# One-core attention and MLP block: reordering the start-up, where V's weights, the first normalised tiles and the first MLP weights are made ready

## The chip, the cores and the metric

The kernel runs on one core of a Trainium2 chip. The core has five engines that run side by side, each with its own queue in program order: TensorE (PE, with weight loads shown apart as PEld), VectorE (DVE), ScalarE (ACT), GpSimd (POOL) and SyncE (SP), which here only issues DMAs. They wait for each other through semaphores. The metric is the device time of one execution in microseconds, lower is better; the number given is the median of several runs.

## What is computed

A layer norm without learned scale, then two branches from the same normalised input, and a gated sum. The input has 4 blocks of 512 tokens and 512 features; each block is handled as four tiles of 128 tokens (`TT = 4`).

```python
xn = layernorm(x, eps=1e-5)                      # (x - mean) / sqrt(var + eps), per token
q, k, v = xn @ wq.T, xn @ wk.T, xn @ wv.T        # 16 query heads, 4 key/value heads of 128
s = lightning_attn(rope(q), rope(k), v) @ wo.T   # linear attention with decay, chunks of 64
gate = silu((xn @ f8(gate_w)) * gate_scale)      # f8: rounded to float8_e4m3fn
up = (xn @ f8(up_w)) * up_scale                  # 1536 hidden features
g = silu(((gate * up) @ f8(down_w)) * down_scale)
out = x + s * g
```

The products are made to float32 accuracy from two parts: every operand is split into a high part (a cast to float32r) and a low part (the value minus its high part), and three products high x high, high x low and low x high are summed (`SPLIT`). For the weights that are exactly float8 values, two products do.

## The kernel before

The program has a long first phase for V and the MLP and a second for attention. The change lies in the first 50 us or so, the start-up, and in nothing else.

**Normalising.** A tile of 128 tokens is loaded (`load_x`), `tile_stats` takes its statistics, `mean_var` aggregates them and adds epsilon for a group of tiles (`LGROUPS`), GpSimd's `power` raises the variance to -1/2, and `inv_std` makes one Newton step of three short instructions on VectorE. `norm` then subtracts and scales in place (L876). TensorE transposes the tile into a PSUM bank (`ln_transpose`, four matmuls against the identity), ScalarE casts it to the high part (`norm_hi`) and VectorE subtracts to make the low part (`norm_lo`). The first eight tiles, two blocks, go through this in the start-up.

**V.** The weights of V come in four slices (`wv_tab`, k = 0 to 3) and are split by `wv_split_hi` on ScalarE and `wv_split_lo` on VectorE. For each of the first four tiles V is summed in three parts of four matmuls: `v_first_high` (high x high), `v_first_low` (low input) and `v_first_rest` (low weights). Tiles 4 to 7 do the twelve in one go (`v_tile`). `v_round` and `v_rest` split the result, and `store_v` writes it to HBM from a ring of slots (`VFIRST`).

**MLP weights.** They come as 12 slabs m = 0 to 11, each with gate, up and down weights; slabs 0 and 1 come in three pieces of 512 columns, the others whole (1536 columns). Rounding to float8 goes: `w_exponent` on VectorE takes the exponent bits into the buffer `mag`, `w_floor` on ScalarE makes them a rounding constant, and `w_round` on VectorE adds and subtracts it (L920, then L925 for gate and up, L929 for down). There is one buffer `mag`, so a slab waits until the one before it has been rounded.

**MLP units.** `gate_up` makes gate and up of one slab for one block in 16 matmuls, `silu_gate` and `fuse` (L937) turn them into the hidden values, `fuse_hi` and GpSimd's `fuse_rest` split these, and `down` uses them two slabs later. Gate and up results rotate through three PSUM banks, and `free_bank` makes TensorE wait until the `silu_gate` or `fuse` of three results ago has read its bank.

The order on each engine is written out by hand, a list of calls per engine; semaphores carry the waits. Warm-up matmuls on zeros (`warm_up`: 14 at the start, 4 more after the first transposes) keep TensorE busy before data is there. The functions that the change touches follow, with the lines of the profile.

## Time and profile before

| | |
|---|---|
| Time, median of 3 runs | 898.89 us (898.34 to 899.41) |
| The profiled execution's own time | 898.42 us |
| Its span in the profile | 896.6 us |
| TensorE busy | 889.5 us, 99% of the span |
| VectorE, ScalarE, GpSimd busy | 655.2, 409.4 and 370.3 us |

The span runs from the first to the last recorded instruction; the execution's own time is 1.8 us longer. The busy time of TensorE is a sum over pipelined matmuls, each shown longer than its distance to the next, so the share says how seldom the engine stands still, not how near it is to its peak.

### The profile page before, as it was taken

The numbers are of one execution on the slowest core, as the hardware profiler recorded it, in microseconds if no ns is written. First come the engines' busy times: TensorE is split into PE (matmuls) and PEld (weight loads), VectorE is DVE, ScalarE is ACT, GpSimd is POOL, SyncE is SP. The second block draws the span as 40 slices with busy tenths as digits, with TensorE's granted clock in tenths as the row PEclk, the third lists the DMA queues.
The fourth block names the chain that finished last, engine by engine and source line by source line (L and its number), as shares of the span: only waits on it lengthen the run. The fifth ranks groups of instructions, "written<-read, shape, count | busy, mean of one in ns | idle before, by whom it ended". The sixth has DMA issues, their size and how long they took to land.

```text
span 896.6 us, 12455 instructions
## 1 busy us (share of the span) xinstructions
PE 889.5 (99%) x4060; PEld 734.0 (82%) x4060; DVE 655.2 (73%) x941; ACT 409.4 (46%) x683; POOL 370.3 (41%) x273
## 2 busy tenths in 40 slices
PE   8999999999999999999999999999999999999998
PEld 5878888888888888888888888888888888888887
DVE  7888896777653257766777867677767678788798
ACT  3443344443533455445355454463554544634432
POOL 1011112122122475636545456365454563553546
PEclk9999999999999999999999999999999999999999
DMA  6694414389650634522534614345335064274844
GB/s 215 201 399 146 170 48 164 142 306 327 246 211 1 212 127 146 185 79 110 187 128 155 224 35 175 102 175 194 103 143 180 19 222 158 100 254 109 293 149 155
DMA packets 86922, 150.08 MB, mean 167 GB/s; under 512 B 38480, under 2 KB 59616, under 8 KB 81504
## 3 DMA queue, kind: packets, MB, share of 16 engines
q1 hardware_dynamic: 86880, 149.55, 48.4%
q8 instruction: 23, 0.38, 0.2%
q14 instruction: 19, 0.16, 0.1%
HBM read 103.38 MB, written 46.15 MB: 167 GB/s over the span
## 4 chain that ended last, share of the span: by engine, by line
PE 90%; DVE 4%; issue 3%; POOL 2%; ACT 1%; DMA 0%; SPq 0%; DVEq 0%; POOLq 0%; ACTq 0%
PE bank L1359 89%; POOL d_r L1295 1%; POOL rot L1304 1%; PE bank L1379 0%; DMA stage<-in_x_nat 0%; DVE d_sb L1151 0%; DVE wst L920 0%; DVE tail_sb L1204 0%; DVE d_sb L1103 0%; DVE tail_sb L1202 0%; DVE d_r L1178 0%; ACT mag L598 0%; DVE acc L1198 0%; PE bank L1415 0%; DVE fz L937 0%
## 5 line engine op out<-in xcount | busy, mean ns | idle before, releaser
L1359 PE MATMUL bank<-xn,aw 128*128 128x512 f32 x960 | 229.1, 390 | 0.0
L1304 POOL TENSOR_TENSOR rot<-rot 128x512 f32<-128x512 f32 x80 | 126.7, 1584 | 233.2 <-DVE rot L1090 233.2
L1359 PEld LDWEIGHTS bank<-xn,aw 128*128 128x128 f32 x960 | 179.0, 188 | 37.3 <-issue 0.7
L1359 PE MATMUL bank<-o_r,ow 128*128 128x512 f32 (+1 forms) x792 | 184.5, 383 | 0.2 <-DVE o_r L1157 0.2
L1295 POOL TENSOR_TENSOR d_r<-d_sb,d_r 128x512 fp32r<-128x512 f32 x126 | 165.6, 1338 | 37.0 <-ACT d_r L762 36.9
L1359 PE MATMUL bank<-xn,gu_w 128*128 128x512 f32 x768 | 179.9, 389 | 0.4 <-DVE fz L937 0.4
L1359 PEld LDWEIGHTS bank<-o_r,ow 128*128 128x128 f32 x792 | 145.5, 188 | 29.8 <-issue 0.6
L1359 PEld LDWEIGHTS bank<-xn,gu_w 128*128 128x128 f32 x768 | 144.1, 188 | 30.7 <-DVE dn_w L929 0.8
L1089 DVE TENSOR_TENSOR rot<-bank,rope 128x512 f32<-128x512 f32 x80 | 55.2, 690 | 100.1 <-ACT rot L747 100.0
L746 ACT COPY rot<-bank 64x512 f32<-64x512 f32 x80 | 46.8, 585 | 156.7 <-PE bank L1359 156.5
L762 ACT CAST d_r<-d_sb 128x512 fp32r<-128x512 f32 x128 | 78.9, 621 | 83.2 <-DVE d_sb L1151 62.3
L1278 POOL TENSOR_TENSOR fsplit<-f_all,fsplit 128x512 fp32r<-128x512 f32 x36 | 49.0, 1367 | 129.1 <-ACT fsplit L620 129.1
L1359 PE MATMUL bank<-fsplit,dn_w 128*128 128x512 f32 x384 | 93.8, 390 | 0.0
L1103 DVE TENSOR_TENSOR d_sb<-rot,q_decay 128x256 f32<-128x256 f32 x64 | 83.6, 1324 | 1.2 <-POOL rot L1304 1.2
L1359 PEld LDWEIGHTS bank<-fsplit,dn_w 128*128 128x128 f32 x384 | 71.8, 188 | 15.5 <-issue 0.3
L1151 DVE TENSOR_TENSOR d_sb<-bank,decay 128x512 f32<-128x512 f32 x96 | 64.0, 684 | 22.5 <-PE bank L1359 21.1
L1359 PE MATMUL bank<-q_r,k_r 128*128 128x512 f32 x288 | 78.4, 391 | 0.0
L1359 PE MATMUL bank<-d_r,v_r 128*128 128x512 f32 (+1 forms) x336 | 76.9, 361 | 0.1
L1359 PEld LDWEIGHTS bank<-d_r,v_r 128*128 128x128 f32 x336 | 57.6, 188 | 13.1 <-POOL d_r L1295 2.3
L1359 PEld LDWEIGHTS bank<-q_r,k_r 128*128 128x128 f32 x288 | 52.9, 188 | 10.7 <-DVE q_r L1096 0.6
L735 ACT CAST q_r<-rot 128x512 fp32r<-128x512 f32 x64 | 39.8, 622 | 40.2 <-POOL rot L1304 39.4
L937 DVE SCALAR_TENSOR_TENSOR f_all<-bank,scale_sb,f_all 128x512 f32<-128x512 f32 x36 | 26.9, 747 | 40.9 <-PE bank L1359 34.9
(91 smaller groups left out, 946.3 us busy)
## 6 DMA issues: line engine op xcount, KB each, us to landing
xn<-xn_split SPq DMA_DIRECT2D x15, 2048.0 KB, 7.7
v_decayed<-vd_split SPq DMA_DIRECT2D x32, 512.0 KB, 3.3
vd_r<-v_decayed SPq DMA_DIRECT2D x16, 1024.0 KB, 7.0
v_r<-v_split SPq DMA_DIRECT2D x16, 512.0 KB, 3.6
wst<-in_mlp_w SPq DMA_DIRECT2D x10, 768.0 KB, 6.0
xn_split<-xn SPq DMA_DIRECT2D x3, 2048.0 KB, 10.5
stage<-in_x_t SPq DMA_DIRECT2D x20, 256.0 KB, 5.1
stage<-in_attn_w SPq DMA_DIRECT2D x4, 1280.0 KB, 5.7
```

The lines of the kernel that those rows point to most:

```text
L735: act.copy(dst, rot1[:, r % RRING, :]).then_inc(qk_hi, 1)
L746: act.copy(rot2[0:ROT, r % RRING, :], ps[ROT:, :])
L762: act.copy(d_r[:, slot(e), 0, :], d_sb[:, slot(e), :]).then_inc(d_hi, 1)
L937: dve.scalar_tensor_tensor(out=f, in0=gu_ps[(2 * u + 1) % 3][:], scalar=scale_sb[:, MT + m:MT + m + 1], in1=f, op0=ALU.mult, op1=ALU.mult) ...
L1089: dve.tensor_tensor(rot1[:, r % RRING, :], proj_bank(n, r)[:], rope[:, 0, :], ALU.mult)
L1103: dve.tensor_tensor(d_sb[:, slot(e), bass.ts(h % 2, HALF)], rot1[:, (h + 1) % RRING, HALF:S], q_decay[:, h, :], ALU.mult).then_inc(q_decay ...
L1151: dve.tensor_tensor(by_head(d_sb[:, slot(e), :]), by_head(sc_ps[t % TRING][:]), decay[:, h0:h0 + nh, i0 - j:i0 - j + ni, :], ALU.mult).the ...
L1278: pool.tensor_tensor(fsplit[:, e % FRING, 1, :], src, fsplit[:, e % FRING, 0, :].bitcast(F32), ALU.subtract).then_inc(f_lo, 1)
L1295: pool.tensor_tensor(d_r[:, slot(e), 1, :], d_sb[:, slot(e), :], d_r[:, slot(e), 0, :].bitcast(F32), ALU.subtract).then_inc(d_lo, 1)
L1304: pool.tensor_tensor(rot1[:, r % RRING, :], rot1[:, r % RRING, :], rot2[:, r % RRING, :], ALU.add).then_inc(qk_sum, 1)
L1359: last = pe.matmul(dst, a, b, start=start and x == 0, stop=stop and x == len(pairs) - 1)
```

## The change

It rearranges the start-up. On SP, V's weight slices are loaded between the first tiles, slab 2 of the MLP weights right after the first slabs, and the tiles of block 2 earlier. On VectorE, the variance group of tiles 0 and 1 becomes two groups of one tile. Three of the eight tiles (3, 6 and 7) are normalised by ScalarE, as x * rstd + (-mean * rstd), for which VectorE makes the new `nmr`. Slabs 1 and 2 get `mag` buffers of their own in `spare`, which lies where block 2's input comes later. V's products of the first tiles are ordered anew on TensorE, with `v_first_rest` taken slice by slice, the four extra warm-up matmuls fall away, and V's ring has six slots in place of four. The rounding of slabs 1 and 2 is interleaved with `fuse` in another order (`FLOW`, `READY`), with `w_round` cut into `w_minus`, `w_out_gu` and `w_out_down`.

```diff
-LGROUPS = [(0, 2), (2, 4), (4, 8), (8, 12), (12, 16)]
+LGROUPS = [(0, 1), (1, 2), (2, 4), (4, 8), (8, 12), (12, 16)]
-VFIRST = 4
+VFIRST = 6
-WARM_MORE = 4
+ON_ACT = (TT - 1, 2 * TT - 2, 2 * TT - 1)
+FLOW = [0, 1, 2, 3, 4, 6, 5] + list(range(7, NPIECES))
...
+        mags = {0: mag[:], 1: spare[:, 0, :], 2: spare[:, 1, :]}
...
@@ sync @@
-            for i in range(TT):
-                load_x(i)
+            load_x(0)
+            load_wv(0)
+            load_x(1)
+            load_wv(1)
             sp.dma_start(ident[:], ident_in).then_inc(ident_sem, 16)
-            for k in range(KT):
-                sp.dma_start(wv_raw[:, k, :], wv_tab[:, k, :]).then_inc(wv_in[k], 16)
-            for i in range(TT, 2 * TT):
+            load_wv(2)
+            load_wv(3)
+            for i in range(2, 2 * TT):
                 load_x(i)
...
-            store_v(0)
             load_w(2)
-            for v in range(1, TT + 1):
+            for v in range(TT + 2):
                 store_v(v)
+            for i in range(2 * TT, 3 * TT):
+                load_x(i)
             load_w(3)
...
@@ scalar @@
+            def norm(i):
+                c = ON_ACT.index(i)
+                act.wait_ge(nmr_d, 1 if c == 0 else 2)
+                act.activation(stage[:, i % XRING, :], stage[:, i % XRING, :], ACT.Identity,
+                               bias=nmr[:, c:c + 1], scale=rstd[:, i:i + 1]).then_inc(normed_act, 1)
...
-            wv_split_hi(0)
+            for k in range(KT - 1):
+                wv_split_hi(k)
             norm_hi(0)
-            for k in range(1, KT):
-                wv_split_hi(k)
-            for i in range(1, TT):
-                norm_hi(i)
+            wv_split_hi(KT - 1)
+            norm_hi(1)
+            norm(TT - 1)
+            norm_hi(2)
+            norm_hi(3)
+            norm(2 * TT - 2)
+            norm(2 * TT - 1)
...
@@ vector @@
+                if grp in (2, 3):
+                    c0, c1 = (0, 1) if grp == 2 else (1, 3)
+                    dve.wait_ge(rstd_d, grp + 1)
+                    dve.scalar_tensor_tensor(out=nmr[:, c0:c1], in0=mv[:, i1 - c1 + c0:i1, 0], scalar=-1.0, in1=rstd[:, i1 - c1 + c0:i1],
+                                             op0=ALU.mult, op1=ALU.mult).then_inc(nmr_d, 1)
...
+            def w_minus(q):
...
+                dve.wait_ge(k_made, FLOW.index(q) + 1)
+                dve.scalar_tensor_tensor(out=wst[:, m % WRING, c0:c1], in0=mag_of(m)[:, c0:c1], scalar=F8_FLOOR,
+                                         in1=wst[:, m % WRING, c0:c1], op0=ALU.add, op1=ALU.subtract).then_inc(k_neg, 1)
...
-            w_exponent(4)
-            for v in range(TT + 2, 2 * TT):
-                v_rest(v)
+            w_exponent(6)
             w_round(4)
             dve.wait_ge(const_in, 16)
             fuse(0, 0)
             w_exponent(5)
+            v_rest(TT + 2)
+            w_minus(6)
+            fuse(1, 0)
+            w_out_gu(6)
+            v_rest(TT + 3)
+            fuse(0, 1)
             w_round(5)
-            w_exponent(6)
-            fuse(1, 0)
-            for m in range(1, MT):
+            w_out_down(6)
+            w_exponent(7)
+            fuse(1, 1)
+            for m in range(2, MT):
...
@@ tensor @@
+            def v_first_rest(k, tiles=range(TT)):
+
+                pe.wait_ge(wv_lo, k + 1)
+                for v in tiles:
+                    mm = pe.matmul(v_bank(v)[:], xn_of(0)[:, 0, k, bass.ts(v, P)], wv[:, 1, k, :], start=False, stop=k == KT - 1)
...
-            warm_up(WARM_MORE)
             v_first_high(0)
+            v_first_low(0)
             v_first_high(1)
+            v_first_rest(0, (0, 1))
+            v_first_low(1)
             ln_transpose(2)
             ln_transpose(3)
-            v_first_low(0)
-            v_first_low(1)
+            v_first_rest(1, (0, 1))
             v_first_high(2)
             v_first_high(3)
             v_first_low(2)
             v_first_low(3)
-            for v in range(TT):
-                v_first_rest(v)
-            for i in range(TT, 2 * TT):
-                ln_transpose(i)
+            v_first_rest(0, (2, 3))
+            v_first_rest(1, (2, 3))
+            v_first_rest(2)
+            ln_transpose(TT)
+            ln_transpose(TT + 1)
+            v_first_rest(KT - 1)
+            ln_transpose(TT + 2)
+            ln_transpose(TT + 3)
```

TensorE's queue at the start, before. L1395 is `warm_up`, L1415 `ln_transpose` (four matmuls a tile), L1379 `v_first_high`, and L1359 the other products of V.

```order
L1415 MATMUL bank<-ident,stage 128x128 x8
L1395 MATMUL bank<-acc 128x512 x4
L1379 MATMUL bank<-wv,xn 128x512 x8
L1415 MATMUL bank<-ident,stage 128x128 x8
L1359 MATMUL bank<-wv,xn 128x512 x8
L1379 MATMUL bank<-wv,xn 128x512 x8
L1359 MATMUL bank<-wv,xn 128x512 x24
L1415 MATMUL bank<-ident,stage 128x128 x16
L1359 MATMUL bank<-wv,xn 128x512 x48
```

The same stretch of the changed kernel, from the end of the second pair of products on; L1481 is `ln_transpose`, L1440 `v_first_high`, L1420 `v_first_low` and later `v_tile`, L1451 `v_first_rest`.

```order
L1440 MATMUL bank<-wv,xn 128x512 x4
L1451 MATMUL bank<-wv,xn 128x512 x2
L1420 MATMUL bank<-wv,xn 128x512 x4
L1481 MATMUL bank<-ident,stage 128x128 x8
L1451 MATMUL bank<-wv,xn 128x512 x2
L1440 MATMUL bank<-wv,xn 128x512 x8
L1420 MATMUL bank<-wv,xn 128x512 x8
L1451 MATMUL bank<-wv,xn 128x512 x8
L1481 MATMUL bank<-ident,stage 128x128 x8
L1451 MATMUL bank<-wv,xn 128x512 x4
L1481 MATMUL bank<-ident,stage 128x128 x8
L1420 MATMUL bank<-wv,xn 128x512 x48
```

Ahead of these rows stand 14 warm-up matmuls, 8 of `ln_transpose`, 4 of `v_first_high` and 4 of `v_first_low`. The number of matmuls of V is the same, 96; four warm-ups are gone, and the last slice's low weights come between the transposes of tiles 5 and 6.

VectorE's queue at the very start, before: L841 is `tile_stats`, L847 and L849 `mean_var`, L857 to L863 `inv_std`, L876 `norm`.

```order
L841 BN_STATS stats<-stage 128x6 x2
L847 BN_AGGR mv<-stats 128x2 x2
L849 TENSOR_SCALAR rs<-mv 128x2
L841 BN_STATS stats<-stage 128x6
L857 TENSOR_TENSOR rs<-rs 128x2
L859 SCALAR_TENSOR_TENSOR rs<-rs 128x2
L863 SCALAR_TENSOR_TENSOR rstd<-rs 128x2
L876 TENSOR_SCALAR stage<-stage,mv,rstd 128x512 x2
```

And in the changed kernel (L873 `tile_stats`, L879 and L881 `mean_var`, L889 to L895 `inv_std`, L913 `norm`).

```order
L873 BN_STATS stats<-stage 128x6
L879 BN_AGGR mv<-stats 128x2
L881 TENSOR_SCALAR rs<-mv 128x1
L873 BN_STATS stats<-stage 128x6
L879 BN_AGGR mv<-stats 128x2
L881 TENSOR_SCALAR rs<-mv 128x1
L889 TENSOR_TENSOR rs<-rs 128x1
L891 SCALAR_TENSOR_TENSOR rs<-rs 128x1
L895 SCALAR_TENSOR_TENSOR rstd<-rs 128x1
L913 TENSOR_SCALAR stage<-stage,mv,rstd 128x512
L889 TENSOR_TENSOR rs<-rs 128x1
```

The statistics of tile 1 still stand ahead of the Newton step and the `norm` of tile 0; what moved is that tile 1's own Newton step now follows the `norm` of tile 0.

VectorE at the first MLP units, before: L913 is `w_exponent`, L920 to L929 `w_round`, L937 `fuse`. The first row is `fuse(0, 0)`, the last `fuse(0, 1)`.

```order
L937 SCALAR_TENSOR_TENSOR fz<-bank,scale_sb,fz 128x512
L913 TENSOR_SCALAR mag<-wst 128x512
L920 SCALAR_TENSOR_TENSOR wst<-mag,wst 128x512
L929 SCALAR_TENSOR_TENSOR dn_w<-mag,wst 128x512
L913 TENSOR_SCALAR mag<-wst 128x1536
L937 SCALAR_TENSOR_TENSOR f_all<-bank,scale_sb,f_all 128x512
L920 SCALAR_TENSOR_TENSOR wst<-mag,wst 128x1536
L925 SCALAR_TENSOR_TENSOR gu_w<-mag,wst 128x1024
L929 SCALAR_TENSOR_TENSOR dn_w<-mag,wst 128x512
L937 SCALAR_TENSOR_TENSOR fz<-bank,scale_sb,fz 128x512
```

And in the changed kernel: L950 is `w_exponent`, L957 `w_minus`, L965 `w_out_gu`, L973 `w_out_down`, L990 `fuse`, L1000 `v_rest`; the first row is again `fuse(0, 0)`.

```order
L990 SCALAR_TENSOR_TENSOR fz<-bank,scale_sb,fz 128x512
L950 TENSOR_SCALAR spare<-wst 128x512
L1000 TENSOR_TENSOR gout<-bank,gout 128x512
L957 SCALAR_TENSOR_TENSOR wst<-spare,wst 128x1536
L990 SCALAR_TENSOR_TENSOR f_all<-bank,scale_sb,f_all 128x512
L965 SCALAR_TENSOR_TENSOR gu_w<-spare,wst 128x1024
L1000 TENSOR_TENSOR gout<-bank,gout 128x512
L990 SCALAR_TENSOR_TENSOR fz<-bank,scale_sb,fz 128x512
L957 SCALAR_TENSOR_TENSOR wst<-spare,wst 128x512
L973 SCALAR_TENSOR_TENSOR dn_w<-spare,wst 128x512 x2
L950 TENSOR_SCALAR mag<-wst 128x1536
L990 SCALAR_TENSOR_TENSOR f_all<-bank,scale_sb,f_all 128x512
```

`fuse(0, 1)` had the whole rounding of slab 2 ahead of it and now has the down piece of slab 1 and of slab 2 behind it; two of V's tiles were split earlier and now stand between.

## Rows read from the trace of the kernel before

**Rows 1.** The page's head and its busy times by engine.

```profile
span 896.6 us, 12455 instructions
PE 889.5 (99%) x4060; PEld 734.0 (82%) x4060; DVE 655.2 (73%) x941; ACT 409.4 (46%) x683; POOL 370.3 (41%) x273
```

**Rows 2.** Chain that ended last, first 100 us: start, length, what.

```profile
51.28 34.74 PE bank L1359 x152
```

**Rows 3.** Timeline of TensorE: start, length, instructions, idle before them and its releaser.

```profile
1.47 5.89 PE L1395 MATMUL bank<-acc 128*128 128x512 bf16 x14 [1.47 <-DVE acc L981]
8.77 1.06 PE L1415 MATMUL bank<-ident,stage 128*128 128x128 f32 x8 [1.41 <-DVE stage L876]
9.67 1.03 PE L1395 MATMUL bank<-acc 128*128 128x512 bf16 x4
10.34 2.96 PE L1379 MATMUL bank<-wv,xn 128*128 128x512 f32 x8
...
25.17 11.18 PE L1359 MATMUL bank<-wv,xn 128*128 128x512 f32 x48
...
51.28 7.54 PE L1359 MATMUL bank<-xn,gu_w 128*128 128x512 f32 x32 [0.42 <-DVE fz L937]
...
60.47 7.42 PE L1359 MATMUL bank<-xn,gu_w 128*128 128x512 f32 x32
67.72 1.98 PE L1359 MATMUL bank<-fsplit,dn_w 128*128 128x512 f32 x8
```

**Rows 4.** TensorE's weight loads, groups by line, 10 to 14 us.

```profile
L1379 PEld LDWEIGHTS bank<-wv,xn 128*128 128x128 f32 x8 | 1.4, 187 | 1.3 <-ACT wv L638 0.7 <-ACT xn L576 0.3
```

**Rows 5.** Stretches: busy us (instructions) of PE, PEld, DVE, ACT, POOL; granted clock; DMA share, GB/s.

```profile
8.77:25.17 16.40, 16.24 (x85) 12.75 (x85) 14.36 (x37) 7.66 (x15) 1.71 (x2) 1.00 0.50 173
25.17:51.28 26.11, 25.69 (x112) 20.98 (x113) 23.11 (x36) 10.91 (x18) 1.29 (x1) 1.00 0.87 269
```

**Rows 6.** Timeline of VectorE, columns as in rows 3.

```profile
3.99 0.69 DVE L841 BATCH_NORM_STATS2 stats<-stage 128x6 f32<-128x512 f32 x1 [2.58 <-DMA stage<-in_x_nat]
5.41 0.69 DVE L841 BATCH_NORM_STATS2 stats<-stage 128x6 f32<-128x512 f32 x1 [0.73 <-DMA stage<-in_x_nat]
...
6.42 0.17 DVE L849 TENSOR_SCALAR rs<-mv 128x2 f32<-128x2 f32 x1
...
7.49 0.16 DVE L857 TENSOR_TENSOR rs<-rs 128x2 f32<-128x2 f32 x1 [0.30 <-POOL rs L1272]
...
8.08 1.00 DVE L876 TENSOR_SCALAR stage<-stage,mv,rstd 128x512 f32<-128x512 f32 x2
...
16.81 2.47 DVE L841 BATCH_NORM_STATS2 stats<-stage 128x6 f32<-128x512 f32 x4
...
58.08 0.95 DVE L913 TENSOR_SCALAR mag<-wst 128x1536 int32<-128x1536 int32 x1
```

**Rows 7.** Timeline of ScalarE, columns as in rows 3.

```profile
8.48 0.62 ACT L638 CAST wv<-f_all 128x512 fp32r<-128x512 f32 x1 [6.46 <-DMA f_all<-in_wv_tab]
9.43 0.59 ACT L576 CAST xn<-bank 128x512 fp32r<-128x512 f32 x1 [0.32 <-PE bank L1415]
...
27.34 1.34 ACT L598 ACTIVATE mag<-mag,floor_b 128x512 f32<-128x512 f32 x2 [1.47 <-DVE mag L913]
```

**Rows 8.** Timeline of GpSimd, columns as in rows 3.

```profile
6.74 0.71 POOL L1272 TENSOR_TENSOR rs<-rs,minus_half 128x2 f32<-128x2 f32 x1 [5.86 <-DVE rs L849]
...
19.97 1.01 POOL L1272 TENSOR_TENSOR rs<-rs,minus_half 128x4 f32<-128x4 f32 x1 [9.02 <-DVE rs L849]
```

**Rows 9.** SP's issues of tiles 1 and 2 (1.2 to 2.0 us).

```profile
L310 SPq DMA_DIRECT2D stage<-in_x_nat x2: 422/422/423, 1.2 to 1.7; - x2
...
DMA to landing us min/median/max: 4.2/4.3/4.4
```

**Rows 10.** SP's issues of slabs 3 and 4 (39 to 46 us).

```profile
L343 SPq DMA_DIRECT2D wst<-in_mlp_w x2: 352/518/685, 39.4 to 45.5; - x2
...
DMA to landing us min/median/max: 5.2/5.6/6.0
```

More of the change, by code:

```diff
@@ L68 @@
 VSLOT = 2
-VFIRST = 4
+VFIRST = 6
+VUSES = [(2 * TT - r + VFIRST - 1) // VFIRST for r in range(VFIRST)]
 SPILL = 4
@@ L85 @@
 WARM = 14
-WARM_MORE = 4
+ON_ACT = (TT - 1, 2 * TT - 2, 2 * TT - 1)
+FLOW = [0, 1, 2, 3, 4, 6, 5] + list(range(7, NPIECES))
+READY = [(0, 0), (0, 1), (1, 0), (1, 1), (0, 2), (2, 1), (1, 2), (2, 2)] + [(m, part) for m in range(3, MT) for part in (1, 2)]
 EXP_MASK = 0x7F800000
@@ L276, in ready @@
         def ready(m, down=False):
-            if m < SLABS:
-                return 2 * SLABS + m + 1 if down else 2 * m + 2
-            return PARTS * SLABS + 2 * (m - SLABS) + (2 if down else 1)
+            return READY.index((m, 2 if down else 1)) + 1
         def slot(e):
@@ L413, in _ @@
             spill_xn(0)
-            for i in range(2 * TT, 3 * TT):
-                load_x(i)
             load_w(5)
@@ L687, in _ @@
             silu_gate(1, 0)
-            w_floor(6)
             for m in range(1, MT):
@@ L999, in _ @@
             norm_lo(3)
+            for i in range(TT, 2 * TT):
+                tile_stats(i)
+            mean_var(3)
             wv_split_lo(2)
             wv_split_lo(3)
-            for i in range(TT, 2 * TT):
-                tile_stats(i)
-            mean_var(2)
-            inv_std(2)
-            for i in range(TT, 2 * TT):
-                norm(i)
+            inv_std(3)
+            norm(TT)
+            norm(TT + 1)
+            norm_lo(TT)
+            norm_lo(TT + 1)
             v_rest(0)
-            for i in range(TT, 2 * TT):
-                norm_lo(i)
+            norm_lo(TT + 2)
+            norm_lo(TT + 3)
             w_exponent(0)
@@ L1279, in fuse_rest @@
                                    ALU.subtract).then_inc(f_lo, 1)
-            power(0)
-            power(1)
-            power(2)
+            for grp in range(4):
+                power(grp)
             for m in range(MT):
@@ L1286, in _ @@
                 if m in GROUP_AT:
-                    power(GROUP_AT[m] + 1)
+                    power(GROUP_AT[m])
             fuse_rest(MT)
```

124 lines of the change are left out of this document (75 added, 49 removed).

## The prediction

> **What bounds the kernel now.** I read the page first, then the chain that ended last, then TensorE's timeline of the start. TensorE is busy for 889.5 of 896.6 us [rows 1], so all the time in which it stands still is 7.1 us, and the change can't win more than a part of that plus the matmuls it removes. The chain shows one unbroken piece of TensorE from 51.28 us on, 34.7 us long [rows 2], and after it the same rhythm goes on: a unit pair and a down product take 60.47 to 67.72 and so on, 32 matmuls in 7.25 us, 0.2266 us each [rows 3]. The change touches only what is made ready before that. So the question is at which time TensorE comes to the row that now starts at 51.28; every later row moves with it.
>
> In the start the reader should see where TensorE loses time [rows 3, 5]. The first transposes start at 8.77, after 1.41 us of waiting for `norm` of tile 0. From 8.77 to 25.17 TensorE has 48 products of V and 32 transposes. The products cost 48 x 0.2266 = 10.9 us; eight transposes take 1.06 us with the tail of the last one, 0.27 long as the others, so they follow each other at 0.113 us and 32 cost 3.6. That is 14.5 of 16.40 us [rows 5]: 1.9 are lost. About 0.9 are the four warm-ups (from the row at 9.67 to the next, at 10.34, and what they push), 1.0 is waiting for ScalarE's casts of V's weights and of tile 1 in the row at 10.34, which takes 2.96 us for 8 products; the weight loads name both releasers [rows 4]. From 25.17 to 51.28 there are 112 products, 25.4 us, in 26.1 [rows 5]: 0.7 is lost, of which 0.42 shows as the wait for VectorE's `fuse(0, 1)` at the end [rows 3]; the rest of the 0.7 I take as partly the same stop, since the end of the matmul ahead is modelled.
>
> **Part 1, the start.** Transfers of 256 KB land in the order of their issue. Tile 0 is first before and after: statistics at 3.99 [rows 6]. Tile 1 moves from second to third place, behind a slice of V's weights. In the trace the second lands for the statistics at 5.41 [rows 6]; the third, issued at 1.7, has the longer landing of the two, 4.4 us, so 6.1 [rows 9]. VectorE still has tile 1's statistics ahead of tile 0's Newton step, so it waits there until 6.1. From statistics to the variance it took 1.01 us with two aggregations (5.41 to 6.42), with one about 0.9: 7.0. GpSimd's power for tile 0 is long done by then: variance at about 4.9, then 0.3 to its start and at most 0.71 [rows 8]. The Newton step follows at once and takes 0.59 (7.49 to 8.08) [rows 6], so `norm(0)` starts at 7.65 where it was 8.08: 0.4 us earlier, and the transposes of tile 0 at 8.35 in place of 8.77. Splitting the group gains only that: the wait of 0.30 for GpSimd [rows 6] goes, and 0.7 of the later landing eats most of the rest of what one tile alone could have given.
>
> Tile 1 pays: its own Newton step now stands behind `norm(0)`, so `norm(1)` is at 7.65 + 0.46 + 0.57 = 8.7 (it was about 8.5), and TensorE, done with tile 0 at 8.8, waits until 9.4. New wait, 0.6.
>
> **Part 2, V's weights and order.** The slices now take places 2, 4, 6 and 7. The sixth place lands at 8.48 (the first slice of before) [rows 7]. ScalarE casts slices 0 to 2 by 9.0, then tile 0's high part, 9.0 plus the 0.9 us that lay between 9.43 and TensorE's next product [rows 3, 7]: 9.9, a wait of 0.1 behind the transposes of tile 1. After that the weights are there, and the 18 products up to `v_first_low(1)` run without the stops of before, to 14.0. The four warm-ups are gone, and the 1.0 of waiting too: 1.9 removed.
>
> **Part 3, the rest of V's first half.** Each new place where VectorE or ScalarE is late, walked with the durations of before. The group of tiles 2 and 3: its statistics stand behind tile 0's low part, its variance at 11.9, GpSimd 0.3 + 0.71, Newton 0.57 and `nmr` 0.1, `norm(2)` 13.65, transposes 14.3: wait 0.3. Then the cast of tile 2 behind its transposes: wait 0.2. The third slice's low part stands behind four statistics (2.47 us, at 16.81 before and about there now) [rows 6] and the aggregation: it is ready at 20.7 against 20.4: wait 0.3. Last, tiles 4 to 7: variance 19.9, GpSimd 1.01 for four columns [rows 8], Newton, `nmr`, `norm(4)` at 21.8, transposes at 22.5, with TensorE there at 21.6: wait 0.9. Here the kernel before had the products of V's low weights in front and no wait. Sum of new waits: 0.6 + 0.1 + 0.3 + 0.2 + 0.3 + 0.9 = 2.4.
>
> So TensorE reaches tile 4's `v_tile` at 8.35 + 14.5 + 2.4 = 25.2, against 25.17. The earlier start (0.4) and the removed 1.9 are used up by the new waits of 2.4, to within 0.1. The reason is that `norm(4)` hardly moves: VectorE is busy for 14.36 of the 16.40 us [rows 5], the same statistics, splits and Newton steps are in front of it, and three normalisations given to ScalarE (0.46 each) save VectorE only what stands behind `norm(2)` and `norm(5)`, plus three small steps more for the extra group and two for `nmr`.
>
> Costs not in the trace. ScalarE's normalisation of a tile with a scale and a bias per partition: below it the cast from SBUF, 0.62, above it an activation with such a bias, (1.34 + 0.10) / 2 = 0.72 [rows 7]; I take 0.72. With either, TensorE is still on tile 2's transposes or waits 0.1 for tile 3; the sum changes by less than 0.1. A power of one column: two cost 0.71 and four 1.01 [rows 8], so 0.56 as a line through both, 0 to 0.71 as bounds; hidden under the wait for tile 1. The Trainium skill (ScalarE: Activation LUTs, Table sets: the hidden batching unit) says that the cheap functions, identity among them, stand in every table set, so no table is loaded for it; no row of before shows an identity, and a load would show as its own row. The same page (What ACT_TABLE_LOAD costs) prices such an activation at an estimated 0.80 us, by which the sum loses 0.02 more.
>
> **Part 4, the second half and the MLP weights.** From 25.2 the 112 products need 25.4 us: 50.6. What made TensorE wait at 51.28 was `fuse(0, 1)` behind the rounding of slab 2; now it stands in front of slab 1's last piece and is done about 3 us before it is needed, and slab 2's gate weights at about 45.4 against 50.6. So the 0.7 is won, if nothing else is late; of it I count 0.6, since small issue gaps were part of it.
> Slab 4 is late next: its load waits for the end of slab 1's rounding, which now comes at about 49.3, so the load moves from 45.5 [rows 10] by 4 us. With the landing of 5.2 to 6.0 us [rows 10] it is there at 54.5 to 55.3; VectorE wants it at about 56.6 (58.08 before) [rows 6]. Cover left: 1.3 us. Behind that wait would stand `fuse(1, 2)`, which TensorE needs only some 5 us later, so a load late by 2 us costs nothing.
>
> **Sum.** 0.0 at 25.2 plus 0.6 at 51 us: 0.6 us. The profiled execution would go from 898.42 to 897.8 (span 896.0), the median, 0.47 above that execution, from 898.89 to 898.3. A change of 0.2% (1.8 us) is about what can be told from none.
>
> **The rivals.**
> A, the forecast: 0.2 to 1.0 us won, 897.9 to 898.7. Chance 0.70.
> B, tile 1 is later than third place suggests, or the weight slices are. If it lands as the fourth, at about 7.2, the transposes start 0.7 us after 8.77 in place of 0.4 before, and the chain behind them shifts: 1.1 us less, so 0.5 lost, 899.4. If it landed as early as 5.4, 0.7 more would be won, 897.6. For it speaks the same bandwidth for all; against it that sizes and places are alike. Chance of the loss 0.12.
> C, the new waits don't come, because VectorE's queue runs ahead more than my walk says. With none of the 2.4 left, 0.6 + 2.4 = 3.0 us are won, 895.9. It needs `norm(4)` at 20.9 or earlier, and VectorE's fill speaks against it. Over 1.8 us: 0.06; between: 0.04.
> D, the other side: TensorE falls to its lower clock. The 14 first warm-ups took 5.89 us, 0.42 each, where V's products of as many columns take 0.23 [rows 3]: that is the level of 1.2 GHz against 2.4, though the granted clock is shown as 1.00 in the later stretches [rows 5]. Before, warm-ups filled the place between the transposes and the first product; now there are stops of 1.0, 0.6 and 0.1 us around eight transposes. If the lower level came back, each product costs 0.2 more: it decides from 9 products on (1.8 us over, with the gain used up, 12), and 20 of them give 4 - 0.6 = 3.4 lost, 902.3. Against it: before, 1.41 us without work ahead of the transposes did not bring it back. Chance 0.05.
> The Trainium skill (TensorE: Matmul & The Clock Gate, What you observe) says that the default is the throttled state and that idleness brings it back; the trace agrees only for the start, and here no longer stop than before is added.
> E, the weights are late: the load of slab 4 and those behind it meet the two spills of 2 MB. From 5 us of lateness on TensorE waits as long as they are late beyond that; 7 us late would cost 2, 900.9. Chance 0.03.
>
> **How the numbers follow.** A, the small part of C, and B lie within 0.2%: 0.86. Faster 0.06 (C), slower 0.08 (D, E). The range takes A, B on both sides, and the spread of the runs shown (about half a microsecond either way): 897.2 to 899.5.
>
> **What would show it.** `norm(0)` at 7.65; a wait of 0.6 between the transposes of tiles 0 and 1; a wait of about 0.9 before those of tile 4; `v_tile` of tile 4 at 25.2; no wait at 51; the 32 products of block 0 and 1 of slab 2 at about 50.6. I am wrong if TensorE reaches `v_tile` before 24.5 or after 26, or if a wait stands in the slabs 2 to 5.

## The result, and the profile after

The changed kernel takes 899.86 us (median of 21 executions, 898.66 to 901.50) against 898.51 for the kernel before in the same comparison (21 executions, 897.84 to 900.11): ratio 1.0014, interval 1.0008 to 1.0020. It is slower by 1.35 us where 0.6 us faster was forecast, and outside the range given (897.2 to 899.5) by 0.4. Five executions in the comparisons below took 1273 to 2631 us, far above all others of the same kernels; they are left out of every median and count here. The profiled execution took 900.24 us, 2.0 more in its span than before [rows 1].

The head of the page after, with the busy times by engine:

```profile
span 898.6 us, 12452 instructions
PE 889.7 (99%) x4056; PEld 734.5 (82%) x4056; DVE 655.9 (73%) x944; ACT 411.5 (46%) x686; POOL 371.6 (41%) x274
```

TensorE has the same work, less four warm-ups, yet the same busy time. Its timeline after (start, length, instructions, idle before them and its releaser):

```profile
1.47 5.98 PE L1458 MATMUL bank<-acc 128*128 128x512 bf16 x14 [1.47 <-DVE acc L1034]
9.77 0.63 PE L1481 MATMUL bank<-ident,stage 128*128 128x128 f32 x4 [2.32 <-DVE stage L913]
10.71 1.12 PE L1481 MATMUL bank<-ident,stage 128*128 128x128 f32 x4 [0.32 <-DVE stage L913]
...
25.16 1.11 PE L1481 MATMUL bank<-ident,stage 128*128 128x128 f32 x8 [0.92 <-DVE stage L913]
...
27.83 11.14 PE L1420 MATMUL bank<-wv,xn 128*128 128x512 f32 x48
38.81 21.92 PE L1420 MATMUL bank<-xn,gu_w 128*128 128x512 f32 x96
```

Four things are to be seen against [rows 3]. The first transposes start at 9.77, not at 8.77 as before, nor at 8.35 as forecast, after a stop of 2.32 us. The second four take 1.12 us where the first four took 0.63. The wait ahead of tile 4's transposes is there, 0.92. And `v_tile` of tile 4 starts at 27.83 against 25.17; from there 144 products run without any wait to past 60, so the wait that stood at 51.28 is gone.

The second of them goes with the granted clock (stretches of after; columns as in [rows 5]):

```profile
9.77:27.83 18.06, 16.74 (x81) 13.28 (x81) 14.01 (x38) 6.78 (x13) 2.09 (x2) 0.91 0.56 194
27.83:53.18 25.35, 25.35 (x115) 21.01 (x114) 24.09 (x36) 13.67 (x22) 3.03 (x2) 1.00 0.80 241
...
10.00:11.00 1.00, 0.68 (x6) 0.44 (x5) 0.96 (x3) 0.57 (x2) 0.00 (x0) 0.78 0.94 352
11.00:12.00 1.00, 1.00 (x5) 0.96 (x4) 1.00 (x3) 0.67 (x3) 0.00 (x0) 0.50 0.63 238
12.00:13.00 1.00, 1.00 (x4) 0.75 (x3) 1.00 (x2) 0.45 (x1) 0.00 (x0) 0.50 0.52 158
13.00:14.00 1.00, 1.00 (x4) 0.81 (x3) 0.93 (x5) 0.00 (x0) 0.38 (x1) 0.52 0.70 162
14.00:15.00 1.00, 1.00 (x5) 0.81 (x5) 0.67 (x5) 0.00 (x0) 0.32 (x1) 1.00 0.62 141
```

The means of 0.78 and 0.52 at the two ends put the fall at about 10.6 and the return at 14.0: for some 3.4 us the clock stands at 0.50, that is 1.2 GHz, and it is back at 1.00 behind. Over the 18.06 us of the first line a mean of 0.91 means 1.6 us of full-speed work not done. The second line, of the second half, is the good part: 25.35 of 25.35 us busy, where before 0.4 of 26.11 were idle [rows 5].

The first thing, the late start, is on VectorE's timeline of after:

```profile
4.82 0.69 DVE L873 BATCH_NORM_STATS2 stats<-stage 128x6 f32<-128x512 f32 x1 [3.40 <-DMA stage<-in_x_nat]
...
7.47 0.69 DVE L873 BATCH_NORM_STATS2 stats<-stage 128x6 f32<-128x512 f32 x1 [1.55 <-DMA stage<-in_x_nat]
...
8.48 0.15 DVE L889 TENSOR_TENSOR rs<-rs 128x1 f32<-128x1 f32 x1
...
9.07 0.55 DVE L913 TENSOR_SCALAR stage<-stage,mv,rstd 128x512 f32<-128x512 f32 x1
```

Tile 0 lands for its statistics at 4.82 (3.99 before, although it is the first transfer in both) and tile 1 at 7.47 (forecast 6.1) [rows 6]. Behind 7.47 everything is as walked, 1.60 us to `norm(0)` where 1.55 was taken: 1.01 us to the Newton step, 0.59 more to `norm(0)` at 9.07. No loading of an activation table was added: the trace of after has one such row, of 1.28 us at 0.75, as the trace of before has at 0.74. ScalarE's normalisation and GpSimd's power of one and of four columns are there for the first time or in a new length:

```profile
15.14 0.82 ACT L592 ACTIVATE stage<-stage,nmr,rstd 128x512 f32<-128x512 f32 x1 [2.69 <-DVE nmr L900]
```

```profile
6.07 0.56 POOL L1334 TENSOR_TENSOR rs<-rs,minus_half 128x1 f32<-128x1 f32 x1 [5.18 <-DVE rs L881]
...
22.48 1.39 POOL L1334 TENSOR_TENSOR rs<-rs,minus_half 128x4 f32<-128x4 f32 x1 [8.16 <-DVE rs L881]
```

The clock is not the same in each execution. Of the 21, sixteen have a mean granted clock of 0.998 or less (median 899.91) and five of 0.999 or 1.000 (median 899.03). Half speed for 3.4 us lowers the mean over the span by 0.0019, so 0.998 is what one such stretch leaves; this is an inference from the mean, as only the profiled execution shows the stretch itself. Three of the sixteen have 0.996 (900.78 to 901.50 us), more than one such stretch leaves; no trace shows what happened in them.

Two theories follow. **Clock**: the longer stop ahead of the first transposes lets TensorE fall to 1.2 GHz, and costs about 1 us. **Landing**: a slice of V's weights between tiles 0 and 1 makes both tiles late, and costs about 0.7 us in the start, whatever the clock. A third question is whether the second half really gives back 0.6. Each experiment below was timed next to the kernel before on the same chip, in three groups, in which that kernel's median was 898.2 (the first four experiments), 898.4 (without the four warm-ups, normalisations undone, one group, wait ahead of tile 4) and 898.2 (the others). In the result above it was 898.51. So a difference between a median below and the changed kernel's 899.86 holds up to 0.3 us that belongs to the comparison and not to the kernel; where it matters, each is also given against its own kernel before.

### The profile page after: what moved, and what is told of

It is laid out like the page before. It is cut to its first block, busy times and chain, and to the rows that moved or that the text cites. A ratio compares the mean times of both kernels' runs of the same rounds, so it can differ in the third digit from the quotient of the medians.

```text
span 898.6 us, 12452 instructions
## 1 busy us (share of the span) xinstructions
PE 889.7 (99%) x4056; PEld 734.5 (82%) x4056; DVE 655.9 (73%) x944; ACT 411.5 (46%) x686; POOL 371.6 (41%) x274
## 4 chain that ended last, share of the span: by engine, by line
PE 90%; DVE 3%; issue 3%; POOL 2%; DMA 1%; ACT 0%; SPq 0%; DVEq 0%; POOLq 0%; ACTq 0%
PE bank L1420 89%; POOL d_r L1356 1%; POOL rot L1365 1%; DMA stage<-in_x_nat 1%; DVE d_sb L1213 0%; PE bank L1481 0%; DVE stats L873 0%; DVE tail_sb L1266 0%; DVE d_sb L1165 0%; DVE tail_sb L1264 0%; DVE d_r L1240 0%; PE bank L1440 0%; DVE acc L1260 0%; DVE stage L913 0%; POOL rs L1334 0%
## 5 line engine op out<-in xcount | busy, mean ns | idle before, releaser
L1420 PE MATMUL bank<-xn,aw 128*128 128x512 f32 x960 | 229.1, 390 | 0.0
L1420 PEld LDWEIGHTS bank<-xn,aw 128*128 128x128 f32 x960 | 179.0, 188 | 37.3 <-issue 0.7
L1420 PE MATMUL bank<-o_r,ow 128*128 128x512 f32 (+1 forms) x792 | 184.5, 383 | 0.2 <-DVE o_r L1219 0.2
L1420 PE MATMUL bank<-xn,gu_w 128*128 128x512 f32 x768 | 179.6, 389 | 0.0
L1420 PEld LDWEIGHTS bank<-o_r,ow 128*128 128x128 f32 x792 | 145.5, 188 | 29.8 <-issue 0.6
L1420 PEld LDWEIGHTS bank<-xn,gu_w 128*128 128x128 f32 x768 | 144.2, 188 | 29.9
L1420 PE MATMUL bank<-fsplit,dn_w 128*128 128x512 f32 x384 | 93.8, 390 | 0.0
L1420 PEld LDWEIGHTS bank<-fsplit,dn_w 128*128 128x128 f32 x384 | 71.8, 188 | 15.5 <-issue 0.3
L1420 PE MATMUL bank<-q_r,k_r 128*128 128x512 f32 x288 | 78.4, 391 | 0.0
L1420 PE MATMUL bank<-d_r,v_r 128*128 128x512 f32 (+1 forms) x336 | 76.9, 361 | 0.1
L1420 PEld LDWEIGHTS bank<-d_r,v_r 128*128 128x128 f32 x336 | 57.7, 188 | 13.1 <-POOL d_r L1356 2.3
L1420 PEld LDWEIGHTS bank<-q_r,k_r 128*128 128x128 f32 x288 | 52.9, 188 | 10.7 <-DVE q_r L1158 0.6
L1340 POOL TENSOR_TENSOR fsplit<-fz,fsplit 128x512 fp32r<-128x512 f32 x12 | 16.7, 1388 | 95.5 <-ACT fsplit L642 95.5
```

Of the source, the lines that this page charges most:

```text
L1340: pool.tensor_tensor(fsplit[:, e % FRING, 1, :], src, fsplit[:, e % FRING, 0, :].bitcast(F32), ALU.subtract).then_inc(f_lo, 1)
L1420: last = pe.matmul(dst, a, b, start=start and x == 0, stop=stop and x == len(pairs) - 1)
```

## The experiments

**More warm-ups.** The changed kernel with 20 warm-ups in place of 14, so that TensorE works for longer and the stop is shorter.

```diff
-WARM = 14
+WARM = 20
```

> The changed kernel with 20 warm-up matmuls at the start in place of 14. Theory 1 (the clock): the profile of the changed kernel shows a stop of 2.3 us ahead of the first transposes and then a granted clock of 0.50 from 10.7 to 14.0 us, 3.3 us at half speed, about 1.6 us lost. Six more warm-ups fill the stop up to about 8.7; the clock stays at 1.00 and the median falls by 1.0 to 1.6 us, to about the time of before (ratio to before 1.000, against 1.0014 for the changed kernel). Theory 2 (the later tiles and the new waits alone are the loss): the clock doesn't matter, the time stays at 1.0014 of before.

Measured: 898.61, ratio 1.0005 (0.9997 to 1.0014); mean clock 0.999 or 1.000 in 10 of 11 executions. Its timeline of TensorE:

```profile
1.48 6.25 PE L1458 MATMUL bank<-acc 128*128 128x512 bf16 x20 [1.48 <-DVE acc L1034]
9.06 0.63 PE L1481 MATMUL bank<-ident,stage 128*128 128x128 f32 x4 [1.34 <-DVE stage L913]
10.02 0.66 PE L1481 MATMUL bank<-ident,stage 128*128 128x128 f32 x4 [0.32 <-DVE stage L913]
...
23.28 1.11 PE L1481 MATMUL bank<-ident,stage 128*128 128x128 f32 x8 [0.92 <-DVE stage L913]
...
25.95 1.39 PE L1420 MATMUL bank<-wv,xn 128*128 128x512 f32 x5
```

Both fours of transposes run at full speed. From 9.06 to 25.95 are 16.89 us; the prediction walked 8.35 to 25.2, 16.85. So without the fall the walk's sum holds to 0.04 us, and the fall costs 18.06 - 16.89 = 1.2 us in the traces. In the medians it is 899.86 - 898.61 = 1.25, or, each against its own kernel before, 1.35 - 0.39 = 1.0. What is left, 0.4 us slower than before where 0.6 faster was forecast, is not the clock.

**Both tiles first.** The changed kernel, with tile 1 ahead of the first slice again.

```diff
             load_x(0)
-            load_wv(0)
             load_x(1)
+            load_wv(0)
             load_wv(1)
```

> The changed kernel with tiles 0 and 1 loaded first, then the four slices of V's weights (the identity after the second slice). Theory 1: tile 1 lands 1 us or more sooner than at 7.44, the first transposes start at about 8.3 to 8.9, the stop ahead of them is short and the clock falls seldom; but the first product waits for ScalarE's cast of the third slice as before, so apart from the clock little is won: 0.8 to 1.6 us under the changed kernel, ratio 1.0000 to 1.0005. Theory 2 (the loss is in the new waits behind 12 us): the first transposes are earlier and the products of V aren't, no gain, 1.0014.

Measured: 897.25, ratio 0.9990 (0.9981 to 0.9999); clock 0.999 or 1.000 in all 11 executions. One line moved, and the kernel is 2.6 us faster than the changed one (2.3, each against its own kernel before), more than the 0.8 to 1.6 expected, and 1.0 faster than the one before. Its timelines of VectorE and of TensorE:

```profile
4.04 0.69 DVE L873 BATCH_NORM_STATS2 stats<-stage 128x6 f32<-128x512 f32 x1 [2.62 <-DMA stage<-in_x_nat]
...
5.05 0.68 DVE L873 BATCH_NORM_STATS2 stats<-stage 128x6 f32<-128x512 f32 x1
```

```profile
7.38 0.66 PE L1481 MATMUL bank<-ident,stage 128*128 128x128 f32 x4 [0.89 <-DMA ident<-in_ident]
...
24.60 11.14 PE L1420 MATMUL bank<-wv,xn 128*128 128x512 f32 x48
```

Tile 1 is there before VectorE asks for it (no idle time ahead of 5.05). The transposes now wait for the identity matrix. The slice behind the two tiles loses nothing: ScalarE casts it at 6.22, in the changed kernel at 6.18.

**Both.** Twenty warm-ups and both tiles first.

> Both: 20 warm-ups and tiles 0 and 1 first. Theory 1: the clock holds, and what is left is the order: the same as the better of the two or up to 0.3 us under it, ratio 0.9995 to 1.000. With 20 warm-ups ending at about 8.7 they may now be in the way of the first transposes by some tenths. Theory 2: 1.0014.

Measured: 897.30, ratio 0.9995 (0.9986 to 1.0004); one execution took 901.26. Timeline of TensorE:

```profile
24.76 11.14 PE L1420 MATMUL bank<-wv,xn 128*128 128x512 f32 x48
```

With the tiles first there is no fall left to prevent, so the extra warm-ups add nothing. This run and the one with late tiles, 20 warm-ups in both and the clock up in both profiles, give the price of the landing by itself: 898.61 - 897.30 = 1.3 us in the medians of one comparison, 25.95 - 24.76 = 1.2 in the start of `v_tile`.

**The second half alone.** The kernel before up to V's first half, and behind it the changed kernel's ring of six slots, its three `mag` buffers, its order of loads from the MLP weights on and its order of rounding.

```diff
-VFIRST = 4
+VFIRST = 6
...
-            v_rest(TT)
             w_exponent(2)
             w_exponent(3)
+            v_rest(TT)
+            w_exponent(4)
...
+            fuse(0, 1)
+            w_round(5)
+            w_out_down(6)
```

> The kernel before in its first 25 us (its loads, groups, casts, normalisation on VectorE, V's order and the four extra warm-ups), with the changed kernel's ring of six, three mag buffers, load order from the MLP pieces on and rounding order behind it. If the MLP part of the change is worth what the traces show at 51 us (0.42 to 0.7 us of stop in front of slab 2's unit, gone in the changed kernel), this is 0.5 to 0.7 us faster than before, ratio 0.9993. If the gain there is an artefact of everything being later in the changed kernel, it is 1.0000, or above it if the later load of slab 4 costs.

Measured: 897.73, ratio 0.9994 (0.9985 to 1.0003), 0.5 us under the kernel before; the interval holds 1, so by the times alone this can't be told from nothing. In its profile nothing waits at 51 us: from `v_tile` of tile 4 to the unit behind the first down products it takes 34.6 us (25.91 to 60.50) where it was 35.3 (25.17 to 60.47 [rows 3]), 0.7 less. But this execution fell to the lower clock too, with the start of the kernel before (timeline of TensorE, then stretches):

```profile
8.67 1.94 PE L1459 MATMUL bank<-ident,stage 128*128 128x128 f32 x8 [2.25 <-DVE stage L899]
...
25.91 11.17 PE L1403 MATMUL bank<-wv,xn 128*128 128x512 f32 x48
36.92 21.92 PE L1403 MATMUL bank<-xn,gu_w 128*128 128x512 f32 x96
...
60.50 1.75 PE L1403 MATMUL bank<-xn,gu_w 128*128 128x512 f32 x7
```

```profile
8.00:9.00 1.00, 0.33 (x2) 0.36 (x3) 1.00 (x3) 0.00 (x0) 0.00 (x0) 0.74 1.04 391
9.00:10.00 1.00, 1.00 (x7) 1.00 (x6) 0.93 (x4) 0.73 (x2) 0.00 (x0) 0.50 1.02 365
```

Here the clock was down by about 8.5, ahead of the first transposes, and eight of them take 1.94 us in place of 1.06. So the start of the kernel before isn't safe from it: three of these 11 executions have a mean of 0.998 or less, and so have 11 of 92 of the kernel before in the three groups. The change made rare into usual.

**The start alone.** The kernel before with the changed kernel's loads, groups, normalisations and product order, and the old second half.

> The kernel before with the changed kernel's first 25 us as they are (loads of V's weights between the tiles, two groups of one tile, three tiles on ScalarE, V's order, no extra warm-ups) and its own MLP part. Theory 1: the whole loss is in the start; the MLP part alone won 0.5 us (ratio 0.9994), so this loses 1.8 to 2.0 us against before: 900.1 to 900.4, ratio 1.0020, with the granted clock under 1.000 in most executions. Rival (the two parts only lose together, by their loads meeting): ratio under 1.0010.

Measured: 902.02 (5 executions, 901.76 to 902.20), ratio 1.0042 (1.0028 to 1.0056); clock 0.998 in all five. That is 1.6 more than the top of what was expected. Timeline of TensorE:

```profile
27.81 11.14 PE L1386 MATMUL bank<-wv,xn 128*128 128x512 f32 x48
...
54.70 6.63 PE L1386 MATMUL bank<-xn,gu_w 128*128 128x512 f32 x28 [1.25 <-DVE fz L962]
```

and of ScalarE and VectorE:

```profile
36.76 0.59 ACT L664 CAST gout<-bank 128x512 fp32r<-128x512 f32 x1 [4.26 <-DMA v_split<-gout]
```

```profile
37.38 0.69 DVE L972 TENSOR_TENSOR gout<-bank,gout 128x512 fp32r<-128x512 f32 x1 [1.07 <-ACT gout L664]
```

`v_tile` is as late as in the changed kernel (27.81), and then the wait for `fuse(0, 1)` is 1.25 where it was 0.42 [rows 3]: with the old order VectorE falls further behind than TensorE does. 27.81 - 25.17 + 0.83 = 3.5, and the span is 3.5 longer. With this start, then, the second half is worth 902.02 - 899.86 = 2.2 in the medians (2.4, each against its own kernel before) and 1.5 in the spans, with the old start 0.5. The last two rows show where VectorE loses the 0.8 more: ScalarE waits 4.26 us until a store of V has freed a slot of the ring, and VectorE, which splits the same tile, waits 1.07 us for ScalarE. In the kernel before ScalarE waited 3.28 for that store and VectorE not at all. The ring has four slots here and six in the changed kernel; that six slots alone would win this back was not tried.

**Tile 1 third, no weights between.** The changed kernel with tiles 0, 2, 1, 3, then the identity and the four slices: it tells whether tile 1 is late by its place or by the slice.

```diff
             load_x(0)
-            load_wv(0)
+            load_x(2)
             load_x(1)
-            load_wv(1)
+            load_x(3)
```

> A probe of landings. The changed kernel with the loads in the order tile 0, 2, 1, 3, identity, then V's four slices: tile 1 stays in third place, but what stands beside it are tiles in place of V's weights. Place theory (the prediction's: the landing goes by place): with tiles 0 and 1 first, tile 0 landed at about 4.0 and a third transfer at 6.1 to 6.2; so the statistics of tile 0 start at 4.0 and those of tile 1 at 6.1. Kind theory (slices of V's weights land slower and hold up the tiles around them, as at 4.8 and 7.5 in the changed kernel): the same 4.0 and 6.1. If it is the distance in place alone that delays them, they start at 4.8 and 7.5 here too. The time is no aim: V's weights come later, about 1 us slower than tiles 0 and 1 first.

Measured: 900.34, ratio 1.0026 (1.0015 to 1.0036); clock 0.998 or less in 7 of 8 executions. Timelines of VectorE and TensorE:

```profile
4.07 0.69 DVE L873 BATCH_NORM_STATS2 stats<-stage 128x6 f32<-128x512 f32 x1 [2.66 <-DMA stage<-in_x_nat]
...
6.45 0.69 DVE L873 BATCH_NORM_STATS2 stats<-stage 128x6 f32<-128x512 f32 x1 [1.28 <-DMA stage<-in_x_nat]
```

```profile
8.75 0.63 PE L1481 MATMUL bank<-ident,stage 128*128 128x128 f32 x4 [2.79 <-DVE stage L913]
```

With a tile as neighbour, tile 0 lands as before and tile 1 in third place at 6.45; with a slice as neighbour 4.82 and 7.47 (4.69 and 6.77 with 20 warm-ups, 5.34 and 7.39 in the start alone). Over all 14 profiles tile 0's statistics start at 3.96 to 4.32 where a tile is issued behind it, and at 4.69 to 5.34 in the three where a slice is. So the place gives about 1 us to tile 1 (6.45 against 5.31 to 5.41 as second), and the slice beside it 0.3 to 1.0 more, and 0.4 to 1.4 to tile 0. A slice by itself is not the slower transfer: third behind two tiles it is cast at 6.22, earlier than the tile in third place here. What goes with the lateness is the rate of the transfers (stretch of after, then of this run):

```profile
3.00:4.50 1.50, 1.50 (x5) 0.52 (x4) 0.00 (x0) 0.00 (x0) 0.00 (x0) 1.00 0.84 146
```

```profile
3.00:4.50 1.50, 1.50 (x6) 0.55 (x4) 0.43 (x1) 0.00 (x0) 0.00 (x0) 1.00 0.77 234
```

In this stretch the three profiles with a slice in second place moved 146 to 153 GB/s, the other eleven 234 to 288. Why the rate drops when tiles and slices take turns is not shown. The time is no better here, 3 us above that with both tiles first where 1 was expected: the clock falls all the same, and ScalarE casts the first slice only at 8.23.

**Fewer warm-ups.** Both tiles first, to bring the fall back without the late landing.

```diff
-WARM = 14
+WARM = 10
```

> Tiles 0 and 1 first (897.25 us) with 10 first warm-ups in place of 14: only the stop ahead of the first transposes grows, by some 1.5 us or less. Theory 1 (a stop of TensorE ahead of the first transposes costs by the clock): executions with a granted clock under 1.000 become the rule, the profile shows a stretch at 0.50 between 5 and 15 us, and the median rises by 0.8 to 1.7 us to 898.0 to 899.0. Theory 2 (the clock is a matter of chance and not of the stop): 897.3.

Measured: 898.26, ratio 0.9998 (0.9989 to 1.0008), 1.0 above the version with 14; clock 0.998 or less in 6 of 10 executions. Its transposes and its stretches:

```profile
7.62 0.63 PE L1481 MATMUL bank<-ident,stage 128*128 128x128 f32 x4 [1.80 <-DVE stage L913]
...
9.41 2.08 PE L1440 MATMUL bank<-wv,xn 128*128 128x512 f32 x4
```

```profile
9.00:10.00 1.00, 0.91 (x4) 0.50 (x2) 0.72 (x2) 1.00 (x3) 0.00 (x0) 0.50 1.05 383
10.00:11.00 1.00, 1.00 (x4) 0.81 (x3) 0.99 (x3) 0.36 (x1) 0.00 (x0) 0.50 1.02 391
11.00:12.00 1.00, 1.00 (x4) 0.81 (x3) 0.93 (x5) 0.00 (x0) 0.04 (x1) 0.50 0.95 258
```

The fall and its price come with fewer warm-ups alone, with early tiles: 6 of 10 executions in place of 0 of 11. Here the clock fell after a stop of 1.80 behind ten warm-ups, while after 1.99 behind fourteen, in the version with one group below, it did not.

**Without the four warm-ups.** The kernel before, less `warm_up(WARM_MORE)`.

> The kernel before without its four extra warm-ups, and nothing else. If they only cost time, it is up to 0.3 us faster (the casts of V's weights are late anyway, so little of the 0.9 us is won) at an unchanged granted clock. If they keep the clock up, the executions with a clock under 1.000 become more frequent than the 12 in 34 of before, and the median rises by 0.5 us or more.

Measured: 898.17, ratio 0.9999 (0.9990 to 1.0008); clock 1.000 in 8 of 11 executions and 0.998 in three, where the kernel before had 0.998 or less in four of 33. The four warm-ups cost no time that can be told; whether they kept the clock up in a few executions, these counts can't tell.

**ScalarE's normalisations undone.** Both tiles first, all eight tiles normalised on VectorE.

> The same base (tiles 0 and 1 first, 897.25 us) with all eight tiles normalised on VectorE as in the kernel before and no nmr. Theory P (giving three tiles to ScalarE is worth next to nothing, as the prediction had it: ScalarE takes 0.8 us for what VectorE does in 0.46, and nmr adds a step): 897.0 to 897.4. Rival (it is a real part of the gain, VectorE being full): 0.5 to 1.0 us slower, 897.8 to 898.2.

Measured: 897.29, ratio 0.9988 (0.9979 to 0.9997), against 897.25 with them. They are worth nothing that can be told.

**One group for tiles 0 and 1.** Both tiles first, variance of the two together.

```diff
-LGROUPS = [(0, 1), (1, 2), (2, 4), (4, 8), (8, 12), (12, 16)]
+LGROUPS = [(0, 2), (2, 4), (4, 8), (8, 12), (12, 16)]
```

> The same base (tiles 0 and 1 first, 897.25 us) with tiles 0 and 1 in one variance group again. With both tiles landed early the split can only move tile 0 by a few tenths, and the first product waits for ScalarE in either form. Theory P: within 0.2 us of 897.25. Rival (the split group is what makes the start early): 0.4 us or more slower.

Measured: 897.45, ratio 0.9990 (0.9981 to 0.9999), 0.2 above 897.25, less than the interval can tell. The clock stayed up in its profile:

```profile
8.20 1.06 PE L1479 MATMUL bank<-ident,stage 128*128 128x128 f32 x8 [1.99 <-DVE stage L913]
```

**The wait ahead of tile 4.** Both tiles first, and statistics of tiles 4 and 5 ahead of the low parts of tiles 2 and 3, since VectorE was idle there.

```diff
             wv_split_lo(1)
+            tile_stats(TT)
+            tile_stats(TT + 1)
             norm_lo(2)
             norm_lo(3)
-            for i in range(TT, 2 * TT):
-                tile_stats(i)
+            tile_stats(TT + 2)
+            tile_stats(TT + 3)
```

> The changed kernel with tiles 0 and 1 loaded first (the faster form of the last runs, 897.25 us), and the statistics of tiles 4 and 5 moved ahead of the low parts of tiles 2 and 3 on VectorE. There VectorE waits 0.77 us for ScalarE's cast, and behind it tiles 4 to 7 are what TensorE waits for (0.92 us ahead of tile 4's transposes, and some 0.3 us for the third slice's low part). Theory W (the new waits behind 12 us are VectorE's queue): the wait falls to about 0.3 and tile 4's products start 0.7 to 0.9 us sooner, median 896.4 to 896.6. Rival (the wait is GpSimd's power or ScalarE, not the queue): no gain, 897.2.

Measured: 896.61, ratio 0.9983 (0.9974 to 0.9992). The wait is 0.43 instead of 0.92 and `v_tile` starts at 23.81 instead of 24.60: the wait really stood on the path. The gain is 0.6 us in the medians and 0.8 when each is taken against its own kernel before, as in the trace.

**The same with 17 warm-ups.**

> The fastest form so far (tiles 0 and 1 first, statistics of tiles 4 and 5 early, 896.61 us) with 17 warm-ups in place of 14, which end at about 7.5, where the first transposes may start at 7.4 to 7.6. Theory 1: the few executions under a clock of 1.000 (3 of 11) go, the median stays within 0.2 us: 896.4 to 896.8. If the warm-ups now delay the first transposes, up to 0.4 us slower.

Measured: 896.41 (896.11 to 896.96), ratio 0.9979 (0.9970 to 0.9988); clock 0.999 or 1.000 in all 11 executions. Timeline of TensorE:

```profile
1.47 5.96 PE L1460 MATMUL bank<-acc 128*128 128x512 bf16 x17 [1.47 <-DVE acc L1034]
8.01 1.09 PE L1483 MATMUL bank<-ident,stage 128*128 128x128 f32 x8 [0.58 <-DMA ident<-in_ident]
...
21.70 1.11 PE L1483 MATMUL bank<-ident,stage 128*128 128x128 f32 x8 [0.44 <-DVE stage L913]
...
24.38 11.18 PE L1422 MATMUL bank<-wv,xn 128*128 128x512 f32 x48
```

This is the fastest version, 1.8 us under the kernel before and 3.5 under the changed one (3.2, each against its own kernel before). Against the version with 14 warm-ups the 0.2 can't be told from nothing, and neither had an execution under 0.999; its slowest execution is at 896.96, not 898.81, but the one at 898.81 had a clock of 1.000.

## Why the prediction was wrong

**Two rivals came together, B (0.12) and D (0.05).** Two steps failed. The first is in Part 1: tile 1 in third place at 6.1, held against rival B because "sizes and places are alike", and so the first transposes at 8.35; tile 1's statistics started at 7.47 and the transposes at 9.77. The second is the argument against rival D: "1.41 us without work ahead of the transposes did not bring it back", and "no longer stop than before is added". The stop ahead of the first transposes was 2.32 us, and the clock fell to 0.50 for some 3.4 us.

The second follows from the first. The stop of 1.0 us that rival D looks at is this one, worked out from the landing of 6.1 (8.35 less the end of the warm-ups at 7.36 [rows 3]). Rival B's own landing would have made it 8.77 + 0.7 - 7.36 = 2.1 us, longer than the 1.41 on which D was put aside, but B was priced by the shift alone and D with the early landing. The chances of the two were given as if they had nothing to do with each other.

**What each cost.** Against the kernel before, 0.6 us faster was forecast and 1.35 slower measured, 1.95 apart. With 20 warm-ups 0.4 slower was measured, so about 1.0 is the clock and 1.0 the landing; the five executions of the changed kernel without a lower mean clock, 0.5 slower than before, say the same. In the traces the two are 1.2 and 1.4 (the start of the transposes, 9.77 - 8.35; with 20 warm-ups it was 9.06, so the landing itself varies). By the bare medians the forecast of 898.3 looks only 0.3 short of the 898.61 with 20 warm-ups, but it was added up from a kernel before at 898.89, which stands at 898.2 beside that run. The clock's price per product was right: about 1.6 us of work is lost at half speed, of which the traces keep 1.2, since some waits are filled, and the sum forecast for it, 20 products and 902.3, was too large; the chance was too small. 10 warm-ups against 14 give the price again, 1.0.

Rival B had the time of 7.2 for tile 1 and forecast a start 0.7 later than 8.77; it was 1.0 later. The rule behind both, that the landing goes by place alone, is what the probe with tile 1 third answers: 6.45 with tiles around it, 6.77 to 7.47 with a slice.

**The walk of Parts 1 to 3, from the first transposes on, was right in its sum.** 16.85 us from the first transposes to `v_tile` of tile 4 were forecast; 16.89 were measured with the clock up. That the sum fits to 0.04 is in part luck. From the start of one row to the next, less 0.113 us for each transpose and 0.2266 for each product, the wait between tiles 0 and 1 is 0.5 where 0.6 stood, the one ahead of tile 2 is 0.3 as forecast, and the two for the third slice and ahead of tile 4 are together 1.45 where 1.2 stood (0.92 of it is idle time in the row). And with the tiles early the same stretch takes 17.22 us (7.38 to 24.60), since the casts of V's weights are then waited for. `v_tile` at 27.83 is past the 26 that the prediction named as its sign of being wrong, for the two reasons above. That the wins of the new order are used up by new waits was right, and moving two statistics wins 0.6 to 0.8 of it back. One reading at the head was wrong: 7.1 us, the span less the busy time, does not bound what can be won, as the 16.40 us in which the prediction itself finds 1.9 lost are shown 16.24 busy [rows 5].

**Part 2.** That four warm-ups and the waits for casts, 1.9 us, go away was right as a sum; the warm-ups by themselves are worth nothing that can be told (898.17 against 898.40); without them the wait for ScalarE's casts grew instead.

**Part 4 was right.** No wait at 51 us, 0.6 counted; 0.7 in the trace and 0.5 in the medians with the old start, the latter not clear of nothing by itself; and the span of the profiled execution is 2.0 longer where `v_tile` is 2.66 later: 0.66. The first product of slab 2's gate had no wait, nor had any of the slabs behind it, so rival E did not come (its 900.9 left out the 0.6 won). Rival C, over-pessimistic waits, did not come either.

**Mis-sized without effect.** ScalarE's normalisation took 0.82 us where 0.72 was taken; the estimate by the Trainium skill (ScalarE: Activation LUTs, What ACT_TABLE_LOAD costs), 0.80, was nearer. A power of one column took the 0.56 of the line through two rows; one of four took 1.39 where 1.01 was taken from [rows 8], which is a part of the wait ahead of tile 4. It took 1.01 in all three profiles with the old start and 1.38 or 1.39 in the eleven with the new one; in the old one VectorE stands idle meanwhile (1.12 us in the kernel before), in the new one it makes low parts of V's weights. No run tells whether that is the cause.

**What stays open.** Which property of the start decides between falling and not: among the 14 profiles, stops of 2.22 us and more (2.22, 2.25, 2.32, 2.79) had a fall, shorter ones, up to 1.99, had none but one, 1.80 behind ten warm-ups. The same kernel shows both in different executions, and the warm-ups themselves take 4.5 to 6.0 us for fourteen. No run here separates the length of the stop from what the warm-ups had done ahead of it: more or fewer warm-ups change both.

## What to carry to other kernels

The length of the first stop on TensorE is a quantity of its own in a start that waits for data: work it out under the late landing as well as under the likely one, and ask which clock the work behind it would get. When two rivals hang on the same quantity, price them together. Compare a forecast as a difference from the kernel before, since the base moves by some tenths of a microsecond between comparisons. In a queue of equal transfers, put those that the first compute needs next to each other, ahead of whatever is needed later; one slice moved between two tiles cost more (2.3 to 2.6 us with all that followed) than the whole change could win. An order that is new in two places is best tested by halves: here the first half lost, the second won, and one line turned the sum around.
